# A gated cross attention block with experts: projection pieces at steps of their own, and a reordered start

## What is computed

```python
x = x + tanh(g_xattn) * attention(layernorm(x), ctx, ctx, wq, bq, wk, bk, wv, bv)   # cross
x = x + tanh(g_ffn) * ffn(layernorm(x))
# ffn(src): q = rope(src @ Wq); k = rope(src @ Wk_c @ Wk); v = src @ Wv_c @ Wv
#           y = rmsnorm(src + softmax(q k^T / 4) v @ Wo)                              # self
#           out = rmsnorm(y + shared expert(y) + two of eight routed experts(y))
```

## Time and profile before

| | us |
|---|---|
| median of 3 runs | 829.59 (827.92 to 831.2) |
| the profiled execution | 824.33 |
| its span, from the first instruction to the last | 822.6 |
| TensorE busy | 749.8 |
| VectorE busy | 535.7 |
| ScalarE busy | 415.6 |

### The profile page before, as it was taken

The page is one execution under the profiler, slowest core; times in us unless marked ns, Lnnn a source line. Parts: engine busy times, 40 slices in busy tenths (PEclk is TensorE's granted clock), DMA queues, the critical chain, the costliest instruction groups (busy, mean ns, idle before and its releaser), DMA issues.

```text
span 822.6 us, 10575 instructions
## 1 busy us (share of the span) xinstructions
PE 749.8 (91%) x3606; PEld 344.0 (42%) x3606; DVE 535.7 (65%) x797; ACT 415.6 (51%) x760; POOL 191.1 (23%) x326
## 2 busy tenths in 40 slices
PE   2978999999999799799889879998999999999994
PEld 2522334234333233234322423422654666448883
DVE  3477884885887887887798788791438312532664
ACT  2626778777775677476567647677211122222000
POOL 2440112303302312301220230010101741400564
PEclk9978999999999999899999999999999999999998
DMA  6492241550540631341153034102300572100011
GB/s 199 141 233 76 60 135 40 154 153 31 165 129 1 186 77 35 118 114 39 39 155 78 1 116 116 40 1 91 116 0 14 204 276 68 61 0 2 26 39 39
DMA packets 51318, 73.33 MB, mean 89 GB/s; under 512 B 6977, under 2 KB 42305, under 8 KB 51265
## 3 DMA queue, kind: packets, MB, share of 16 engines
q1 hardware_dynamic: 47936, 63.93, 27.6%
q0 software_dynamic: 2816, 8.46, 2.7%
q10 hardware_dynamic: 512, 0.26, 0.1%
HBM read 45.04 MB, written 27.33 MB: 88 GB/s over the span
## 4 chain that ended last, share of the span: by engine, by line
PE 65%; DVE 14%; ACT 5%; DMA 5%; POOL 4%; issue 3%; SPq 2%; ACTq 0%; DVEq 0%; POOLq 0%
PE ps L1356 30%; PE ps L1474 11%; PE ps L1494 11%; PE ps L1446 9%; DVE negm L1027 5%; PE ps L1351 2%; DMA w<-scrk 2%; POOL scrf L667 2%; DVE qk L952 2%; ACT hS L811 2%; ACT rows L738 1%; DVE bst L931 1%; PE ps L1462 1%; DMA scrk<-mix 1%; PE ps L1454 1%
## 5 line engine op out<-in xcount | busy, mean ns | idle before, releaser
L1027 DVE TENSOR_REDUCE negm<-ps 128x2 f32<-128x1024 f32 x256 | 301.8, 1222 | 48.4 <-PE ps L1446 43.3
L811 ACT ACTIVATE hS<-ps 128x512 f32<-128x512 f32 x512 | 274.7, 599 | 102.8 <-PE ps L1494 101.1
L1446 PE MATMUL ps<-w 96*128 96x512 bf16 x512 | 159.3, 394 | 19.4 <-DVE hS L1046 11.3
L1494 PE MATMUL ps<-w 98*128 98x512 bf16 x512 | 163.8, 391 | 6.5 <-ACT hS L811 3.0
L1474 PE MATMUL ps<-hS,mix 128*17 128x512 f32 x1024 | 137.8, 610 | 0.2
L1494 PEld LDWEIGHTS ps<-w 98*128 98x128 bf16 x512 | 40.5, 98 | 161.7 <-ACT hS L811 83.4
L1446 PEld LDWEIGHTS ps<-w 96*128 96x128 bf16 x512 | 48.4, 100 | 78.8 <-DVE negm L1027 16.7
L1212 DVE SCALAR_TENSOR_TENSOR ctxs<-qk,ps 128x512 f32<-128x512 f32 x32 | 22.0, 688 | 73.0 <-ACT qk L845 72.5
L845 ACT ACTIVATE qk<-ps 128x512 f32<-128x512 f32 x32 | 19.1, 597 | 82.5 <-PE ps L1356 78.6
L1356 PE MATMUL ps<-w,hS 128*128 x256 | 55.7, 380 | 2.0 <-issue 2.0
L1356 PEld LDWEIGHTS ps<-w,hS 128*128 128x128 f32 x256 | 48.6, 190 | 9.3 <-issue 2.8
(11 more groups left out here) (206 smaller groups left out, 866.5 us busy)
## 6 DMA issues: line engine op xcount, KB each, us to landing
w<-scrq SPq DMA_DIRECT2D x32, 384.0 KB, 4.1
scrq<-mix SPq DMA_DIRECT2D x16, 384.0 KB, 3.3
scrk<-mix SPq DMA_DIRECT2D x24, 256.0 KB, 2.2
scrq<-mix SPq DMA_DIRECT2D x24, 256.0 KB, 2.7
w<-scrk SPq DMA_DIRECT2D x32, 192.0 KB, 4.5
w<-scrk SPq DMA_DIRECT2D x32, 128.0 KB, 4.4
w<-in_L_ffn_W_experts_dram SPq DMA_DIRECT2D x8, 512.0 KB, 8.1
mix<-scrf SPq DMA_DIRECT2D x4, 528.0 KB, 6.6
```

What stands on the lines that cost most here:

```text
L811: nc.scalar.activation(prob[:, kt % PROB_SLOTS, s % HG, :], slot_bank(("unit", u)), ACT.Exp, scale=SC).then_inc(s_exp, 1)
L1027: V.tensor_reduce(negm[:, gi % 2, 2 * t2:2 * t2 + 2, h], ps[:, bank:bank + 2, :], AX.X, ALU.max, negate=True).then_inc(s_re, 1)
L1446: last = MM(ps[:, bank + t, :], qs[0:STK, g, h, tt * P:(tt + 1) * P], ks[0:STK, g, h, :], start=True, stop=True)
L1494: MM(take(("unit", u)), ks[:, g, h, kt * P:(kt + 1) * P], qs[:, g, h, :], start=True, stop=True).then_inc(s_sT, 1)
```

## The change

1. **Pieces at steps of their own.** `HOOKS` is filled from three tables, `CROSS_STEPS`, `SELF_STEPS` and `FA_STEPS`. Each entry is (what, piece, step), the step counted from the start of attention n = m-1 and often negative. `tile` is TensorE's filling of a piece, `empty` the emptying of it by its owner, `norm` a half of the normed rows; `part0`, `rest`, `part1`, `part2` and `sum` are the steps of the split. A projection's pieces now lie from step -16 to step +9 around the attention's beginning instead of at step 23.
2. **Work given from VectorE to others.** For self attentions the sum that ends the rotation goes to GpSimd (`rotated_sum`), part 0's cast to ScalarE (`first_part`), and the rest of the keys to GpSimd (`rest`).
3. **The start.** SyncE loads x, the context, then wk, wq, wv with a semaphore each; the context of batch 1 goes to a buffer of its own; the five biases are loaded from ScalarE's queue. The keys of m = 0 are made, split and stored ahead of the queries (`BEGIN`). Part 0 comes straight from PSUM (`begin_parts`) and so does the rest (`begin_rest`). The tanh comes behind all this, and `setup` (the ffn weights' reordering on VectorE) moves to step 8 of the loop. The first six pieces of m = 1 follow at once, its queries and values between the first eight pairs of row maxima.
4. **Stores.** SyncE stores the parts of m = 1 only when the first group's maximum rows have landed. Stacks load keys first and wait for the queries' scratch apart.
5. The 1.0 rows of the keys' stacks are set by GpSimd in two halves, one of them ahead of the first statistics.

```diff
-    for n in range(NI):
+    CROSS_STEPS = [("stats", 0, -34), ("norm", 1, -20), ("norm", 0, -16), ("tile", 2, -12), ("empty", 2, -12), ("tile", 0, -11),
+        ("empty", 0, -11), ("tile", 3, -10), ("empty", 3, -10), ("tile", 1, -6), ("empty", 1, -6), ("tile", 4, -5),
+        ("empty", 4, -5), ("tile", 5, -5), ("empty", 5, -5), ("tile", 6, -4), ("empty", 6, -4), ("part0", 0, -3),
+        ("part1", 0, 1), ("rest", 0, 1), ("empty", 8, 2), ("tile", 8, 2), ("part2", 0, 2), ("tile", 7, 3),
+        ("empty", 7, 3), ("part0", 1, 3), ("rest", 1, 4), ("tile", 9, 5), ("empty", 9, 5), ("part1", 1, 7),
+        ("part2", 1, 10)]
+    SELF_STEPS = [("stats", 0, -28), ("norm", 0, -21), ("norm", 1, -20), ("tile", 0, -14), ("empty", 0, -14), ("tile", 1, -9),
+        ("empty", 1, -8), ("tile", 4, -4), ("empty", 2, -3), ("empty", 4, -3), ("tile", 2, -3), ("tile", 3, -2),
+        ("empty", 3, -2), ("tile", 5, -1), ("empty", 5, 0), ("sum", 0, 1), ("tile", 6, 2), ("empty", 6, 2),
+        ("sum", 1, 2), ("tile", 7, 5), ("empty", 7, 5), ("part0", 0, 5), ("rest", 0, 5), ("tile", 8, 7),
+        ("empty", 8, 7), ("rest", 1, 8), ("part2", 1, 8), ("part0", 1, 10), ("part1", 0, 14), ("part2", 0, 14),
+        ("part1", 1, 16)]
+    FA_STEPS = [("fatile", 0, 12), ("faempty", 0, 12), ("faempty", 1, 15), ("fatile", 1, 15), ("faempty", 2, 19), ("fatile", 2, 19),
+        ("fatile", 3, 23), ("faempty", 3, 23), ("fastats", 0, 32), ("nf", 0, 43)]
...
+    BEGIN = [2, 3, 6, 7, 0, 1, 4, 5, 8, 9]
...
             load_x(0)
-            for s_, d_ in ((src[0], wq), (src[1], wk), (sa[0], wv)):
-                sp.dma_start(s_[:, 0:CT, :], d_.rearrange("(o p) c -> p o c", p=P)).then_inc(s_wn, 16)
-            load_ctx(0)
+            load_ctx(0, ctxs[:])
+            for j in (1, 0, 2):
+                sp.dma_start(WRAW[j], (wq, wk, wv)[j].rearrange("(o p) c -> p o c", p=P)).then_inc(s_wn[j], 16)
             load_x(1)
+            load_ctx(1, sa[1])
...
             stack(0)
-            stack(1)
             next_ctx(2)
             load_x(2)
             load_x(3)
+
+            sp.wait_ge(s_mrow, 16 * MPART)
+            stack(1)
...
+            def rotated_sum(m, X):
+                pool.wait_ge(s_rot[X], SELF_NO[m])
+                link(pool.tensor_tensor(qk[X][:], qk[X][:], rb[X], ALU.add))
+                pool.sem_inc(s_sum[X], 1)
...
+            def begin_parts(m, X):
+                ge(act, s_scr[X], m * SCR[X])
+                for o in range(2):
+                    nc.scalar.activation(parts[X][:, 0, o, :], full(("proj", m, 4 + 2 * X + o)), ACT.Identity,
+                                         bias=bqk[:, X, o:o + 1]).then_inc(s_p0[X] if o else s_hp[X], 1)
+
+            def begin():
+                cross_tile(0, 2)
+                cross_tile(0, 3)
+                normalise(0, 0)
+                normalise(0, 1)
+                begin_parts(0, 1)
+                cross_tile(0, 0)
+                cross_tile(0, 1)
+                begin_parts(0, 0)
...
+            act.wait_ge(s_wb, 16 * N_BIAS)
+            begin()
+            act.wait_ge(s_ws, 16 * N_SMALL)
+            nc.scalar.activation(tg[:], gates[:], ACT.Tanh).then_inc(s_tg, 1)
+            begin_second()
...
+            def begin_rest(m, X):
+                ge(dve, s_spl[X], m)
+                for o in range(2):
+                    dve.wait_ge(s_p0[X] if o else s_hp[X], m + 1)
+                    V.scalar_tensor_tensor(out=qk[X][:, o, :], in0=full(("proj", m, 4 + 2 * X + o)), scalar=bqk[:, X, o:o + 1],
+                                           in1=parts[X][:, 0, o, :], op0=ALU.add, op1=ALU.subtract).then_inc(s_tv, 1)
...
             for q in range(LEAD):
                 if q == PAIRS // NG + 1:
                     turn_max(0)
                 max_pair(q)
+
+                if q < 4:
+                    second_query(*divmod(q, 2))
+                elif q < 8:
+                    second_value(*divmod(q - 4, 2))
```

More of the change, by code:

```diff
@@ new lines, in flamingo_block @@
+    FA_STEPS = [("fatile", 0, 12), ("faempty", 0, 12), ("faempty", 1, 15), ("fatile", 1, 15), ("faempty", 2, 19), ("fatile", 2, 19),
+        ("fatile", 3, 23), ("faempty", 3, 23), ("fastats", 0, 32), ("nf", 0, 43)]
+    SELF_NO = {m: sum(k_ == "s" for k_, _ in INST[:m + 1]) for m in range(NI)}
+    for n in range(1, NI):
+        m = n + 1
+        if m < NI:
+            for what, i, step in (CROSS_STEPS if INST[m][0] == "c" else SELF_STEPS):
+                hook(n, step, what, m, i)
+        if INST[n - 1][0] == "s":
+            for what, i, step in FA_STEPS:
+                hook(n, step, what, INST[n - 1][1], i)
@@ L325, in flamingo_block @@
         s_ldx = [sem(f"x_loaded{i}") for i in range(B)]
[L326 removed]
+        s_ldc = [sem(f"ctx_loaded{i}") for i in range(B)]
         s_src = sem("normed_ready")
@@ L562, in _ @@
             link(pool.memset(mhalf[:], -0.5))
+            pool.memset(stacks[96:P, 1, NG // 2:], 1.0).then_inc(s_one, 1)
+            pool.wait_ge(s_one, 1)
             def row_scale(b, kind):
@@ L646, in _ @@
             stats(1)
-            pool.memset(stacks[96:P, 1], 1.0).then_inc(s_one, 1)
-            pool.wait_ge(s_one, 1)
-            split(1)
+            pool.memset(stacks[96:P, 1, 0:NG // 2], 1.0).then_inc(s_one, 1)
+            pool.wait_ge(s_one, 2)
+            for X in (1, 0):
+                rest(1, X)
+                third_part(1, X)
+            pool.wait_ge(s_tg, 1)
             constants()
@@ L656, in _ @@
                             add_heads(group_inst(gi - 1)[1], (gi - 1) % NG)
-                        for stage, m in HOOKS.get((n, g, s), []):
-                            if stage == "stats":
+                        for what, m, i in HOOKS.get((n, g, s), []):
+                            if what == "stats":
                                 stats(m)
-                            elif stage == "proj":
-                                split(m)
-                            elif stage == "fa":
+                            elif what == "sum":
+                                rotated_sum(m, i)
+                            elif what == "rest":
+                                rest(m, i)
+                            elif what == "part2":
+                                third_part(m, i)
+                            elif what == "fastats":
                                 row_scale(m, "y")
@@ L818, in _ @@
                             max_rows(gi + 1)
-                        for stage, m in HOOKS.get((n, g, s), []):
-                            if stage == "norm0":
-                                normalise(m, 0)
-                            elif stage == "norm1":
-                                normalise(m, 1)
-                            elif stage == "proj":
-                                project(m)
-                            elif stage == "second":
-                                second_part(m, 1)
-                            elif stage == "fa":
-                                turned_attention(m)
+                        for what, m, i in HOOKS.get((n, g, s), []):
+                            if what == "norm":
+                                normalise(m, i)
+                            elif what == "empty" and OWNER[INST[m][0]][i] == "A":
+                                (cross_tile if INST[m][0] == "c" else self_tile)(m, i)
+                            elif what == "part0":
+                                first_part(m, i)
+                            elif what == "part1":
+                                second_part(m, i)
+                            elif what == "faempty" and OWNER["fa"][i] == "A":
+                                turned_attention(m, i)
             copy_values(GROUPS - 1)
```

396 lines of the change are left out of this document (230 added, 166 removed).

## The result

| | before | after |
|---|---|---|
| median of 4 runs | 829.07 us (827.92 to 831.2) | 796.47 us (794.84 to 799.23) |
| the profiled execution | 824.33 | 799.23 |
| its span | 822.6 | 797.5 |
| TensorE busy | 749.8 | 752.8 |
| VectorE busy | 535.7 | 512.8 |

After to before is 0.9607 (95% interval 0.9571 to 0.9643): the kernel is 32.6 us faster. The forecast was 43 us. The time lies inside the range of 774 to 802, and 10 us above the point. They can be split in three stages at the first and the last copy of a group's output (`copy_values`): the first copy starts at 80.92 us before and 69.89 after, 11.0 won in the start; from first to last copy it is 490.11 and 470.68, 19.4 won in the loop; behind it 251.57 and 256.93, 5.4 lost.

What follows compares the result with a forecast made beforehand. TensorE was taken to bound the loop, a chain of loads and stores the start; 32 us in the loop plus 11 in the start gave 43, so 829.6 - 43 = 786.6 us, range 774 to 802.

Steps and rivals of the forecast that it cites:

- (b): Start: only 3 us won, as biases land late and stores and loads compete; 794.6 us; 0.12 together with the clock case.
- (c): Start: the lead before the first units begins at the lower clock, costing 8 us; 794.6 us; 0.12 together with the late-bias case.
- The start: Stretch up to the first unit: earlier biases, stores and maximum rows, less added work, win 11 us; bounds 6 and 15.
- The price of that overlap: Start: VectorE's cast to part 1 meets GpSimd's memset and takes 2.04 us; without overlap the sum is 1.35 better.
- the sum of 36.7: Start: last store, landing, one issue and load put the first pair of row maxima at 36.7 us, rounded to 36.
- The gain of 1.8: Start: the maximum rows' DMA lands in 2.5 us, not 4.27, with the stores of m = 1 behind it.
- The loop: Attention loop: spreading pieces among units leaves 10 of 42.4 us of waste, so 32 us won; bounds 16 and 42.4.
- the 42.4 us of waste: Loop: total of window time above four bare groups and the priced projections and outputs.
- Rival (a): Loop: TensorE waits 0.6 us at each of 26 pieces VectorE empties, winning only 16 there; 802.6 us; chance 0.13.
- Some 2.5 us: Loop before the change: the rest of a self projection's loss, put down to matmuls at the lower clock level.
- The stacks' chain: Loop: GpSimd's queue ends at step 23, loads at 37, before the first row maximum at 41; costs nothing, 3 us room.
- the rival: Loop: stacks come late in every attention, at step 41; slower kernel if 7 us beyond the room; chance 0.03.

Runs made afterwards that it cites:

- e9_halves2: Changed kernel with VectorE's statistics and scalings cut in halves, self statistics at steps -34 and -30: 795.68 us, loop 467.84.
- e0_after: The changed kernel run once more, unedited: median 797.34 us, loop 470.76.
- e7: Changed kernel with the stores of m = 1 no longer waiting for the first maximum rows: 796.35 us, loop 470.75.
- e2: Changed kernel with key and value pieces in neighbouring slots, at steps 5 and 7, in self attentions: 802.12 us, loop 476.44.
- e10: Changed kernel with key and value pieces paired, value first, at steps 5 and 10, later key split steps moved back: 796.73 us, loop 469.7.
- e8: Changed kernel with all pieces of each projection in one burst at step 7, outputs' at 13: 808.23 us, loop 481.15.
- e11: Changed kernel with later bias wait, halved statistics, key and value pieces paired, and cross pieces in a burst at step 7: 789.01 us, loop 464.4.
- e1: Changed kernel with all pieces of each projection in one burst at step 23, outputs' at 13: 854.8 us, loop 526.1.
- e3: Changed kernel with only the cross projections' pieces in a burst at step 23: 804.59 us, loop 478.53.

## Why the prediction came out as it did

**Sign and order of size: right.** Both terms exist. What is short is the loop's. The time, 796.5, is 9.9 above the forecast and 1.9 above the 794.6 of rivals (b) and (c), neither of which happened.

**The start, 11 expected and 11.0 found.** That it fits so well is luck. The biases landed at 10.9 instead of 11.6, but the key product took 5.41 instead of 3.5. At 12 to 24 us the granted clock was 0.86; in e9_halves2 it was 1.00 and the product 3.71, but in e0_after the profile shows 1.00 as well and the product took 6.18, so the clock that the rows show is not the whole cause, and it stays open. The cast behind the queries took 0.73 and not 2.04, since GpSimd's memset of the second half came only at 27.36 us, behind it. The price of that overlap was taken from the earlier trace rows and never came up, so after does not test the rule of the Trainium skill on the shared interface that stood beside it ("Advanced Engine Details and Errata", GPSIMD Details) at that place. The first pair did not wait for the load on which the sum of 36.7 ends, but for TensorE's work on m = 1. And the start of the same code put the first pair between 33.2 and 38.5 in other runs. From the first pair to the copy of the turned maxima it took 12.7 us, 11.1 before: the pieces between the pairs cost 1.6, where 1 was put. The gain of 1.8 behind it was 1.75, for a reason that e7 leaves open. The lead ran at full clock: rival (c) did not happen between 36 and 48 us. The lower level came right behind it, at the first units, as in the kernel before. Windows of after:

```profile
42.00:48.00 6.00, 5.51 (x28) 3.76 (x27) 5.50 (x8) 1.51 (x2) 3.29 (x2) 1.00 1.07 300
48.00:54.00 6.00, 3.92 (x13) 1.04 (x11) 5.83 (x8) 2.25 (x4) 2.40 (x3) 0.68 0.39 128
```

**The loop, 32 expected and 19.4 found.** The step that failed is the reckoning of the 42.4 us of waste, and of what stays of it: "What stays: ... I take 1.5 us per window for six windows and 1 for the outputs, 10 us". With the prediction's own prices for the work (12.3, 9.5 and 4.5) the excesses of after leave 15.1 - 12.3 = 2.8 twice, 13.2 - 9.5 = 3.7 twice, and 43.5 - 2 x 9.5 - 3 x 4.5 = 11.0, together 24 us and not 10. (By the same account before has 43.3: its last output leaves 2.0 and not 1.)

Only half of these 24 us is idle time. The windows of the whole loop show 12.1 us of it, close to the 10. The other 11.8 is time in which TensorE is busy beyond those prices, and before has 11.6 of it. The prediction took all that a window has above its prices as waste that can be won, and named only 2.5 of the busy part, for the lower clock. But the busy column of the earlier trace rows (60.60 of 66.74, 64.98 of 72.10) already gave 6.1 and 7.1 of idle time where it reckoned 8.6 and 9.5 of waste. Idle time was 31.7, and 19.6 of it went.

What the experiments show of the 24:

- VectorE's lumps. The step took them from the cross windows of before, with VectorE elsewhere at ease. One lump costs 0.92 in its interval (13.07), and splitting all of them brought 2.8 us (e9). Busy sums per window (59.34 in 72) say nothing on this; the two bank pairs of the row maxima do.
- Key and value pieces that stand alone leave half of the array idle, 0.93 a pair, 7.4 us in all. In the burst of before they partly ran beside each other: by the earlier trace rows the four take from 406.08 to 409.76 with 0.59 of waiting, 3.1, against 4.2 alone. So 1.1 a self projection, 4.4 in the loop, is work that the change made dearer; the prediction priced a piece as the same wherever it stands. The busy time of the loop did not grow by this much, since the share at the lower clock went at the same time. That the matmul time can be won is shown (e2, e10), and that it then comes back as waits, too.
- The cross pieces. A dense burst at step 7 costs 0.8 above its 12.3, spread pieces 2.8 (e8). Of these 2 us the lump of statistics makes up some 0.55 (e9). The rest was not taken apart; spread pieces stand between units with other weights.

By size these are 2.8 + 4.4 + 4.0 less the 1.1 of the cross statistics that is in two of them, 10.1 of the 12.6 that were missing. That is a sum of parts and not a measured whole: undone together they gave 6.3 (e11), and most of what the pairs win goes, by the listed waits, into the blocked casts.

**The waits at VectorE's pieces.** Rival (a) put 16 us on the loop, and 19.4 is nearer to it than to 32. But its mechanism is not it: 0.6 at each of 26 pieces was its price, and the listed waits on `qk` are 1.9 us in 4. The loop came near to (a) for another reason.

**The clock.** "Some 2.5 us" of the loop at lower clock before fits: the whole loop has 0.98 before and 1.00 after, with no wait longer than 0.9. The 2.5 itself was not measured.

**The stacks' chain.** Right in after: no wait of TensorE on a stack in the loop. That the margin is real and small is shown by e1 and e3, in which the same chain starts at step 23 and TensorE waits up to 8.5 and 3.8. I gave the rival 0.03 since after starts it early; the early start, not GpSimd's low load, is what keeps it off (e8, from step 7, waits for no stack of queries either).

**The experts' stage.** Expected as long as now; in the profile it is 5.4 us longer with the same instructions. In kernels here that leave it alone it lasts 252.0 to 257.0 us, and the one trace of before has 251.57. The window of e3_cross_burst, against the last of after above:

```profile
547.16:799.20 252.04, 235.20 (x902) 159.15 (x902) 109.38 (x256) 41.08 (x71) 76.96 (x95) 0.98 0.21 75
```

The count of matmuls is equal, their busy time differs by 3.7 us, and the granted clock is 0.98 and 0.97 (0.99 in before). It varies from execution to execution; what brings the clock down there was not settled. Start and loop (11.0 + 19.4 = 30.4) stand against 32.6 in the medians, and this variation is larger than what is between them.

## What to carry to other kernels

Give pieces of other work places of their own only where their emptying, and not their density, costs time: here it paid 2 to 4.4 us for each self projection, which waited for its emptying, and lost 2 for a cross projection, which didn't. Take as what can be won the idle time of the bound engine, and not all that a stretch has above the price of its work: 31.7 us against 43.3 here. Look at the longest uninterrupted stretch of the engine that empties against the depth of the ring between it and the bound engine, not at its busy share: 1.4 us of statistics against one spare bank pair cost 0.9 us, with VectorE busy for 44.96 of that window's 63.68. When work is given to a slower engine, follow the last result of its queue to the load that needs it, and move the start by as much: pieces laid from step -16 on, or all at step 7, made TensorE wait for no stack of queries, and pieces at step 23 made it wait 37 us.

## What the runs showed of the hardware

- Two float32 matmul pieces of 64 rows each ran side by side when they stood next to each other in the queue (1.17 us for both), and one after the other's full time with a unit in between (1.05 each).
- Work moved from VectorE to GpSimd took 2.35 us instead of 1.23 for a 128x1024 sum, and the rest 2.13. Before, the rest on VectorE took 2.92 beside GpSimd, 1.23 otherwise and 2.35 in the mean, so for this one GpSimd is not slower. The two rows of groups, GpSimd in after and VectorE before:

```profile
L636 POOL TENSOR_TENSOR qk<-qk,mix 128x1024 f32<-128x1024 f32 x12 | 25.6, 2130 | 36.8 <-ACT mix L811 36.5 <-POOL rows L652 0.4
```

```profile
L952 DVE TENSOR_TENSOR qk<-qk,mix 128x1024 f32<-128x1024 f32 x6 | 14.1, 2352 | 20.8 <-ACT mix L749 20.2
```

- A small cast on VectorE that began beside a 128x1024 operation of GpSimd ended with it: 1.5 to 1.8 us for 0.17 (e10_pairs2, eight times). Beside a 128x4 operation it took its 0.17.
- A stretch of the same code differs between executions by more than is measured here. The first pair of an unchanged start came between 33.18 (e9_halves2) and 38.52 us (e0_after), through the key product (3.71 and 6.18 us, with a granted clock of 1.00 in the rows of both) and through the load of the first stack, 4.37 in the one and 6.77 in the other. The experts' stage took 252.0 to 257.0. The loop of after, which keeps TensorE busy without a wait over 0.9 us, repeats to 0.1.
- Behind a wait of 3.81 us of TensorE in an otherwise full stretch a pair of matmuls took 1.03 instead of 0.60 for some 6 us (e3_cross_burst), and the same showed within 3 us behind a wait of 1.30 (e2_pairs).
